# Reading the convolution taps from PSUM, with two more input products on GpSimd, in a graph layer and state-space kernel on one core

## The chip, the core and the metric

The kernel runs on one core of a Trainium2 chip. TensorE (PE in the profile) multiplies matrices into PSUM and loads its weights in parallel (PEld); VectorE (DVE), ScalarE (ACT) and GpSimd (POOL) work on tensors in SBUF, the first two on PSUM too; SyncE (SP) issues transfers. Each engine runs its own list of instructions in order, and the engines meet only at semaphores. The metric is the device time of one execution in microseconds (us), lower is better.

## What is computed

64 sequences of 128 tokens with 256 features pass through a graph layer and a Mamba block, both with a residual. Everything is fp32.

```python
x = x + relu(sum_k Xk @ Wk[k] + bk[k])       # graph layer: Xk = transition @ Xk-1, on layernorm(x)
h = layernorm(x) @ W_fc1.T + b_fc1            # Mamba block, inner width 1024, 16 states
u, z = split(h @ W_in.T)
u = silu(sum(u_pad[:, k:k+L] * conv_w[:, k] for k in range(4)) + conv_b)    # u_pad: 3 zeros ahead
dt, B, C = split(u @ W_xproj.T);  delta = softplus(dt @ W_dt.T + b_dt)
h_t = exp(delta_t * A) * h_t-1 + delta_t * u_t * B_t;  y_t = sum_s h_t * C_t
x = x + fc2(((y + u * D) * silu(z)) @ W_out.T)
```

## The kernel before

**Tiles and stages.** The 64 sequences are 32 pairs; a pair has 256 columns (2 x 128 tokens), and its 1024 inner channels are 8 blocks `j` of 128 partitions. The state recurrence of one pair is cut into 32 units `v`: a unit is two blocks (i = v // 8) times two of the 16 states, 1024 elements for each partition. For each unit, the input product du x B is written to one of eight slots of `st`, by VectorE (`inject`, line 879) or for the units in `POOL_UNITS` by GpSimd (line 388); ScalarE writes the decays exp(delta x A) to one of two PSUM buffers `dec` (four activations, line 467); VectorE runs the recurrence over `st` (`scan_unit`, line 891); GpSimd multiplies by C (`c_product`, line 404); TensorE sums over the states into `y_ps` (`state_sum`, line 699).

**Software pipeline.** Each engine walks the same list: `body(k)` runs units 0 to 31 of pair k, and between them the dense stage of pair k+1 and the graph stage of pairs k+2 and k+3, at fixed unit numbers. Two bodies make one iteration of a hardware loop. Inside a body the order on each engine is written out by hand; nothing is scheduled.

**The dense stage** of pair k+1, by unit. TensorE projects u, two blocks at a time, into the two halves of the one bank `d_ps` (line 739, in `U_STEPS`). One unit later ScalarE copies a block with its bias into a zero-padded SBUF buffer `upad` (line 510) and writes the newest tap's product to `u` (line 513). VectorE then adds the three older taps out of `upad`: 24 operations for a pair (`tap`, line 912), two behind each scan in units 2 to 13. SiLU of u follows in unit 14 (line 526), the x projection in 15 and 16, dt in 18 to 24 (`abs`, `relu`, lines 539 and 540), exp in 22 and 26, ln in 27 (line 550), z in 26 to 29 (lines 751 and 522). SiLU of z is in unit 6 of the pair's own body (line 484). SiLU, ln and exp each need another function table on ScalarE. GpSimd then makes delta (line 370) and delta x u (line 378).

**What holds what.** `d_ps` is one bank for u, x, dt and z: the next projection waits until the last one is read out. In units 2 to 13 `c_product` waits on semaphore `taps` until the two taps behind that unit's scan are done; at two graph operations it waits likewise. `gate` (line 898, in units 2, 10, 18 and 26) reads `y_ps` after the last state sum of a block pair, and TensorE can't start the next block pair's sum (line 695, then 699) before it. `POOL_INJECTS` says after which `c_product` GpSimd makes which unit's input product; `POOL_DELTAS` and `POOL_DUS` do so for lines 370 and 378.

Of the kernel before, what the change touches and what calls it, by code (L numbers as in the profile page):

```python
# [30 lines left out]
UPADS = 6  # L31
# [16 lines left out]
FOLD_OUT = {9: 0, 10: 3, 11: 1, 13: 2}  # L48
# [13 lines left out]
def build(nc, x, adjT, w_inT, w_fc1, w_out, w_fc2T, w_vT, aw, bv, ab, wk, bk, b_fc1, conv_w, conv_b,  # L62
# [5 lines left out]
    with ExitStack() as ctx:  # L68
# [258 lines left out]
        def _(pool):  # L327
            def body(pool, k, p, scan, dense, ends, begins):
                r = 1 - p
                for v in range(U):  # L330
# [61 lines left out]
            def c_product(pool, k, p, v, steps, dense):  # L392
# [3 lines left out]
                if dense and 2 <= v < 2 + (TAPS - 1) * JP:  # L396
                    wait(pool, "taps", (TAPS - 1) * J * (k + 1) + 2 * (v - 2) + 2)
# [14 lines left out]
        def _(act):  # L412
# [60 lines left out]
            def body(act, k, p, scan, dense, ends, begins):  # L473
# [3 lines left out]
                for v in range(U):  # L477
# [11 lines left out]
                    if isinstance(k, int) and k == 0:  # L489
                        fold_wo(act, v)  # L490
# [8 lines left out]
            def dense_act(act, g, r, v):  # L499
                if v - 1 in U_STEPS:  # L500
# [106 lines left out]
        def _(pe):  # L607
# [58 lines left out]
            def body(pe, k, p, scan, dense, ends, begins):  # L666
                r = 1 - p
                for v in range(U):
# [6 lines left out]
                    if isinstance(k, int) and k == 0:  # L675
                        fold_wo(pe, v)
# [359 lines left out]
```

## Time and profile before

| | us |
|---|---|
| median of 3 runs (4177.37 to 4192.95) | 4181.41 |
| the profiled execution's own time | 4176.09 |
| its span, first to last instruction | 4174.3 |
| VectorE busy | 3766.7 (90%) |
| TensorE busy | 3575.7 (86%) |
| GpSimd busy | 3326.2 (80%) |
| ScalarE busy | 2976.9 (71%) |

In the views below a group's row gives source line, engine, operation, what it writes and reads, shapes and count, then busy time in us and mean nanoseconds of one, then the engine's idle time before the group and what ended it. Engines overlap a little from one instruction to the next, so an instruction occupies its engine slightly less than its duration; the distance from one start to the next shows it. Granted TensorE clock over the span was 0.96 of full speed.

### The profile page before, as it was taken

The page shows a single profiled execution, that of the slowest core. Times are in us where ns is not written, and L with a number is a line of the kernel's source. Part 1 is how long each engine was busy: PE and PEld are TensorE (multiplying, and loading weights), DVE is VectorE, ACT ScalarE, POOL GpSimd, SP SyncE. Part 2 cuts the span into 40 slices and gives each one's busy share as a digit, 9 for nine tenths or more (in the row PEclk, how much of TensorE's full clock was granted, in tenths as well). Part 3 has the DMA queues.
Part 4 walks back from the last instruction along what each step waited for, and adds up shares of the span by engine and source line. Part 5 has one row for each costly group of instructions (what it writes and reads, how often), then busy time and mean ns, then how long its engine had stood idle before and what let it go on. Part 6 is the DMA issues. An engine that isn't in the chain of part 4 may idle for free.

```text
span 4174.3 us, 45057 instructions
## 1 busy us (share of the span) xinstructions
PE 3575.7 (86%) x11386; PEld 2016.6 (48%) x11386; DVE 3766.7 (90%) x3219; ACT 2976.9 (71%) x6358; POOL 3326.2 (80%) x1764
## 2 busy tenths in 40 slices
PE   6688889888888888889888888888889888888887
PEld 3454555444545444545444445444545444555443
DVE  0399999999999999999899999999999999999998
ACT  1577777777777777777777777777777777777764
POOL 0287878888888888888888888888878888788888
PEclk9799999999999999999999999999999999999999
DMA  2111001111101111101111101111101111101110
GB/s 96 47 50 53 36 29 43 50 52 52 39 25 44 49 52 52 52 12 43 50 52 52 52 12 44 49 52 52 51 12 43 50 52 52 39 25 43 46 46 8
DMA packets 50716, 183.79 MB, mean 44 GB/s; under 512 B 7339, under 2 KB 33203, under 8 KB 42067
## 3 DMA queue, kind: packets, MB, share of 16 engines
q1 hardware_dynamic: 48880, 174.17, 11.0%
q10 hardware_dynamic: 1636, 7.83, 0.5%
q14 instruction: 182, 1.49, 0.1%
q8 instruction: 18, 0.29, 0.0%
HBM read 164.15 MB, written 17.83 MB: 44 GB/s over the span
## 4 chain that ended last, share of the span: by engine, by line
PE 32%; DVE 23%; ACT 19%; issue 17%; POOL 6%; DVEq 1%; DMA 0%; ACTq 0%; POOLq 0%; SPq 0%
PE y_ps L699 15%; DVE st L891 11%; ACT dec L467 8%; PE d_ps L751 4%; DVE st L879 4%; POOL st L404 4%; DVE u L912 3%; PE y_ps L695 3%; PE d_ps L762 2%; ACT L467 2%; PE d_ps L739 2%; PE d_ps L773 2%; DVE zs L898 2%; ACT delta L550 1%; ACT zs L522 1%
## 5 line engine op out<-in xcount | busy, mean ns | idle before, releaser
L404 POOL TENSOR_TENSOR st<-st,bc 128x1024 f32<-128x1024 f32 x1024 | 2403.4, 2356 | 642.7 <-DVE u L912 373.5
L891 DVE TENSOR_TENSOR_SCAN st<-dec,st 128x1024 f32<-128x1024 f32 x1024 | 2327.5, 2279 | 176.9 <-ACT dec L467 174.9
L467 ACT ACTIVATE dec<-delta,decay 128x254 f32<-128x254 f32 x4096 | 1700.6, 467 | 797.1 <-DVE st L891 791.1
L699 PE MATMUL y_ps<-st,ident 128*128 128x512 f32 x4096 | 2023.1, 624 | 242.3 <-POOL st L404 237.3
L699 PEld LDWEIGHTS y_ps<-st,ident 128*128 128x128 f32 x4096 | 770.2, 197 | 1025.9 <-issue 612.6
L879 DVE TENSOR_TENSOR st<-du,bc 128x1024 f32<-128x1024 f32 x800 | 963.5, 1204 | 36.2 <-ACT du L453 35.9
L388 POOL TENSOR_TENSOR st<-du_sb,bc 128x1024 f32<-128x1024 f32 x224 | 528.6, 2360 | 0.1
L912 DVE SCALAR_TENSOR_TENSOR u<-upad,chan,u 128x256 f32<-128x256 f32 x768 | 392.3, 551 | 6.4 <-ACT u L513 6.4
L695 PE MATMUL y_ps<-u,diag 128*128 128x256 f32 x512 | 157.6, 434 | 209.7 <-DVE zs L898 209.7
L751 PE MATMUL d_ps<-xnT,wxz 128*128 128x256 f32 x1024 | 254.7, 393 | 62.9 <-ACT zs L522 62.2
L751 PEld LDWEIGHTS d_ps<-xnT,wxz 128*128 128x128 f32 x1024 | 198.3, 196 | 161.7 <-ACT zs L522 103.3
L721 PE MATMUL g<-wo,zs 128*128 128x256 f32 x1024 | 248.7, 386 | 0.8 <-DVE zs L898 0.8
L739 PE MATMUL d_ps<-xnT,wxz 128*128 128x256 f32 x1024 | 244.5, 382 | 1.1 <-ACT u L513 0.9
L721 PEld LDWEIGHTS g<-wo,zs 128*128 128x128 f32 x1024 | 196.0, 194 | 98.8 <-issue 76.6
L739 PEld LDWEIGHTS d_ps<-xnT,wxz 128*128 128x128 f32 x1024 | 196.5, 192 | 82.4 <-issue 60.8
L695 PEld LDWEIGHTS y_ps<-u,diag 128*128 128x128 f32 x512 | 91.9, 199 | 287.3 <-DVE zs L898 279.2
L370 POOL TENSOR_TENSOR delta<-delta,relu 128x512 f32<-128x512 f32 x128 | 162.3, 1268 | 35.4 <-ACT delta L550 35.1
L522 ACT ACTIVATE zs<-d_ps,bxz 128x256 f32<-128x256 f32 x256 | 106.5, 466 | 99.6 <-PE d_ps L751 99.6
L510 ACT ACTIVATE upad<-d_ps,bxz 128x256 f32<-128x256 f32 x256 | 120.0, 469 | 71.8 <-PE d_ps L739 71.8
L378 POOL TENSOR_TENSOR du_sb<-delta,u 128x512 f32<-128x512 f32 x128 | 162.6, 1271 | 0.1
L539 ACT ACTIVATE delta<-d_ps,chan 128x256 f32<-128x256 f32 x256 | 120.9, 472 | 41.7 <-PE d_ps L773 40.0
L773 PE MATMUL d_ps<-dbc,rows 32*128 32x256 f32 x512 | 145.0, 402 | 5.1 <-ACT relu L540 5.1
(105 smaller groups left out, 2831.2 us busy)
## 6 DMA issues: line engine op xcount, KB each, us to landing
bc<-bc_dram SPq DMA_DIRECT2D x64, 2048.0 KB, 9.6
xg<-x_dram SPq DMA_DIRECT2D x32, 256.0 KB, 2.8
x_dram<-xg SPq DMA_DIRECT2D x32, 256.0 KB, 2.0
last_x<-x_dram SPq DMA_DIRECT2D x32, 256.0 KB, 2.6
out_dram<-last_x SPq DMA_DIRECT2D x32, 256.0 KB, 2.2
bc<-w_inT_dram ACTq DMA_DIRECT2D x1, 4096.0 KB
adjt<-adjT_dram SPq DMA_DIRECT2D x32, 128.0 KB, 2.5
bc<-w_out_dram ACTq DMA_DIRECT2D x1, 2048.0 KB
```

The lines of the kernel that those rows point to most:

```text
L388: nc.gpsimd.tensor_tensor(st[:, sl, :, :, :], du_sb[:, None, :, :].to_broadcast([P, SU, 2, T]), bc[:, r, 0, SU * q:SU * q + SU, None, :].t ...
L404: nc.gpsimd.tensor_tensor(st[:, sl, :, :, :], st[:, sl, :, :, :], bc[:, p, 1, SU * q:SU * q + SU, None, :].to_broadcast([P, SU, 2, T]), AL ...
L467: a = nc.scalar.activation(dec[:, v % 2, s, j, :].rearrange("p (b t) -> p b t", b=PAIR)[:, :, 1:], delta[:, p, 2 * i + j, :].rearrange("p ...
L695: nc.tensor.matmul(y_ps[:, j, :], diag[:, 2 * i + j, :], u[:, p, 2 * i + j, :], start=(j == 0), stop=False, skip_group_check=True)
L699: mm = nc.tensor.matmul(y_all, ident[:, :], st[:, sl, s, :, :].rearrange("p j t -> p (j t)"), start=False, stop=(q == Q - 1 and s == SU - ...
L721: mm = nc.tensor.matmul(o_ps[:, b, :], zs[:, p, j, b * L:(b + 1) * L], wo[:, j, :], start=False, stop=(j == J - 1), skip_group_check=True)
L739: mm = nc.tensor.matmul(d_ps[:, j % 2, :], wxz[:, c, j * P:(j + 1) * P], xnT[:, r, c, :], start=(c == 0), stop=(c == KC - 1))
L751: mm = nc.tensor.matmul(d_ps[:, j % 2, :], wxz[:, c, INNER + j * P:INNER + (j + 1) * P], xnT[:, r, c, :], start=(c == 0), stop=(c == KC - 1))
L773: mm = nc.tensor.matmul(d_ps[:, j % 2, :], wdt[:, j * P:(j + 1) * P], dbc[0:RANK, :], start=True, stop=True)
L879: nc.vector.tensor_tensor(st[:, sl, :, :, :], du[:, None, :, :].to_broadcast([P, SU, 2, T]), bc[:, p, 0, SU * q:SU * q + SU, None, :].to_b ...
L891: nc.vector.tensor_tensor_scan(h, dec[:, v % 2, :, :, :].rearrange("p s j t -> p (s j t)"), h, 0.0, ALU.mult, ALU.add).then_inc(S["scanned ...
L912: nc.vector.scalar_tensor_tensor(dst, upad[:, j % UPADS, :, m:m + L], chan[:, m, j:j + 1], dst, ALU.mult, ALU.add).then_inc(S["taps"], 1)
```

## The change

The taps no longer read `upad`. They read the projection where TensorE left it, in `d_ps`, and `upad` with its ScalarE copy (8 for a pair) is gone. Since nothing is padded there, a tap that is `late` tokens behind covers 128 - `late` columns of each sequence. The bias of the projection is folded into one constant for a channel (`bconv`), and the first three tokens, for which that is too much, get one correcting addition of 48 elements a partition at the end (`edge`). All six taps of two blocks now stand behind one scan, in units 1, 3, 5 and 7, and the next u projection waits for them (`taps`) and not for ScalarE (`u_biased`).

With it: the wait on `taps` in `c_product` is dropped; u's last projection is in unit 6 instead of 7; SiLU of u in 9 instead of 14; the x projection in 11 and 12 instead of 15 and 16; dt in 14 to 20; exp in 18 and 22; ln in 24; SiLU of z in 3 instead of 6. GpSimd makes nine input products instead of seven (units 4 and 12 are added), VectorE 23 instead of 25. Folding W_out and fc2 into one matrix, done once, moves from the first pair's units to the body before it, and VectorE copies the results.

```diff
-POOL_UNITS = (0, 8, 16, 20, 24, 27, 30)
-POOL_INJECTS = {5: 8, 13: 16, 17: 20, 20: 24, 24: 27, 26: 30}
-POOL_DELTAS = {2: 1, 9: 2, 11: 3}
-POOL_DUS = {4: 1, 12: 2, 18: 3}
+POOL_UNITS = (0, 4, 8, 12, 16, 20, 24, 27, 30)
+POOL_INJECTS = {0: 4, 5: 8, 8: 12, 12: 16, 16: 20, 20: 24, 23: 27, 26: 30}
+POOL_DELTAS = {2: 1, 9: 2, 14: 3}
+POOL_DUS = {4: 1, 11: 2, 18: 3}
...
-U_STEPS = (0, 2, 4, 7)
+U_STEPS = (0, 2, 4, 6)
 Z_STEPS = (26, 27, 28, 29)
-SILU_U, SILU_Z = 14, 6
+X_STEPS = (11, 12)
+DT_STEPS = (14, 16, 18, 20)
+EXP_STEPS = (18, 22)
+LN_STEP = 24
+SILU_U, SILU_Z = 9, 3
...
                 wait(pool, "scanned", U * k + v + 1)
-                if dense and 2 <= v < 2 + (TAPS - 1) * JP:
-                    wait(pool, "taps", (TAPS - 1) * J * (k + 1) + 2 * (v - 2) + 2)
...
                     for j in (2 * i, 2 * i + 1):
-                        nc.scalar.activation(upad[:, j % UPADS, :, TAPS - 1:],
-                                             d_ps[:, j % 2, :].rearrange("p (b t) -> p b t", b=PAIR),
-                                             ACT.Identity, bias=bxz[:, j:j + 1])
                         nc.scalar.activation(u[:, r, j, :], d_ps[:, j % 2, :], ACT.Identity, bias=bconv[:, j:j + 1],
                                              scale=chan[:, TAPS - 1, j:j + 1]).then_inc(S["u_biased"], 1)
...
-                        wait(pe, "u_biased", J * g + 2 * i)
+                        wait(pe, "taps", CONV * g + 6 * i)
...
-            def tap(dve, g, r, v):
-
-                if not 2 <= v < 2 + (TAPS - 1) * J // 2:
-                    return
-                i, m = (v - 2) // (TAPS - 1), (v - 2) % (TAPS - 1)
...
-                    nc.vector.scalar_tensor_tensor(dst, upad[:, j % UPADS, :, m:m + L], chan[:, m, j:j + 1], dst,
-                                                   ALU.mult, ALU.add).then_inc(S["taps"], 1)
+            def conv(dve, g, r, v):
+
+                for i, start in enumerate(U_STEPS):
+                    for n in range(6):
+                        if v == start + 1:
+                            tap(dve, g, r, i, n)
+                if v == U_STEPS[3] + 1:
+
+                    wait(dve, "taps", CONV * (g + 1) - 1)
+                    first = u[:, r, :, :].rearrange("p j (b t) -> p j b t", b=PAIR)[:, :, :, 0:TAPS - 1]
+                    nc.vector.tensor_tensor(first, first, edge[:, :, None, :].to_broadcast([P, J, PAIR, TAPS - 1]),
+                                            ALU.add).then_inc(S["taps"], 1)
+
+            def tap(dve, g, r, i, n):
+
+                m, j, late = n // 2, 2 * i + n % 2, TAPS - 1 - n // 2
+                if m == 0:
+                    wait(dve, "u_biased", J * g + 2 * i + 2)
+                else:
+                    wait(dve, "taps", CONV * g + 6 * i + n - 1)
+                dst = u[:, r, j, :].rearrange("p (b t) -> p b t", b=PAIR)[:, :, late:]
+                src = d_ps[:, j % 2, :].rearrange("p (b t) -> p b t", b=PAIR)[:, :, 0:L - late]
+                nc.vector.scalar_tensor_tensor(dst, src, chan[:, m, j:j + 1], dst, ALU.mult, ALU.add)\
+                    .then_inc(S["taps"], 1)
```

VectorE in the first scanning body, from the scan of unit 2 on before the change, and from the scan of unit 1 on after it. `st<-du,bc` is an input product, `st<-dec,st` a scan, `u<-...` the taps. Before:

```order
L891 SCALAR_TENSOR_TENSOR st<-dec,st 128x1024
L912 SCALAR_TENSOR_TENSOR u<-upad,chan,u 128x256 x2
L879 TENSOR_TENSOR st<-du,bc 128x1024
L891 SCALAR_TENSOR_TENSOR st<-dec,st 128x1024
L912 SCALAR_TENSOR_TENSOR u<-upad,chan,u 128x256 x2
L879 TENSOR_TENSOR st<-du,bc 128x1024
```

After:

```order
L866 SCALAR_TENSOR_TENSOR st<-dec,st 128x1024
L898 SCALAR_TENSOR_TENSOR u<-d_ps,chan,u 128x2x125 x2
L898 SCALAR_TENSOR_TENSOR u<-d_ps,chan,u 128x2x126 x2
L898 SCALAR_TENSOR_TENSOR u<-d_ps,chan,u 128x2x127 x2
L854 TENSOR_TENSOR st<-du,bc 128x1024
L866 SCALAR_TENSOR_TENSOR st<-dec,st 128x1024 x2
L898 SCALAR_TENSOR_TENSOR u<-d_ps,chan,u 128x2x125 x2
```

Twos behind every scan became sixes behind every second one, the first of them a unit earlier; the two scans in a row are units 2 and 3, since unit 4's input product went to GpSimd.

ScalarE at the same place, from the decays of unit 2 on (`dec<-` x4 is one unit's decays; L513, now L500, writes the newest tap; L477 is SiLU of z). Before:

```order
L467 ACTIVATE dec<-delta,decay 128x2x127 x4
L510 ACTIVATE upad<-d_ps,bxz 128x2x128
L513 ACTIVATE u<-d_ps,bconv,chan 128x256
L510 ACTIVATE upad<-d_ps,bxz 128x2x128
L513 ACTIVATE u<-d_ps,bconv,chan 128x256
L467 ACTIVATE dec<-delta,decay 128x2x127 x4
L590 ACTIVATE xn<-g 128x512
```

After:

```order
L460 ACTIVATE dec<-delta,decay 128x2x127 x4
L500 ACTIVATE u<-d_ps,bconv,chan 128x256 x2
L460 ACTIVATE dec<-delta,decay 128x2x127 x4
L577 ACTIVATE xn<-g 128x512
L460 ACTIVATE dec<-delta,decay 128x2x127 x4
L500 ACTIVATE u<-d_ps,bconv,chan 128x256 x2
L477 ACT_TABLE_LOAD
L477 ACTIVATE zs<-zs 128x2048
L460 ACT_TABLE_LOAD
```

The copies to `upad` are gone, and SiLU of z with its two table loads now stands in unit 3, behind the second pair of u writes.

## Rows read from the trace of the kernel before

**Rows 1.** The page, busy time of each engine, share of the span, instructions.
```profile
PE 3575.7 (86%) x11386; PEld 2016.6 (48%) x11386; DVE 3766.7 (90%) x3219; ACT 2976.9 (71%) x6358; POOL 3326.2 (80%) x1764
```
**Rows 2.** Ln, once a pair, whole span, then to 3800 us: ns min/median/max, first and last start.
```profile
L550 ACT ACTIVATE delta<-delta x32: 1910/1911/1912, 177.0 to 4040.1; 128x2048 f32<-128x2048 f32 x32
...
L550 ACT ACTIVATE delta<-delta x29: 1910/1910/1912, 177.0 to 3678.9; 128x2048 f32<-128x2048 f32 x29
```
**Rows 3.** Waits over the span: engine, line, waited for; us in total, times, longest.
```profile
POOL st L404 <- DVE u L912: 373.5, 279, 3.0
PE y_ps L695 <- DVE zs L898: 209.7, 126, 4.2
DVE st L891 <- ACT dec L467: 174.9, 138, 4.3
...
ACT du L453 <- issue: 26.3, 13, 2.3
```
**Rows 4.** Groups of VectorE instructions over the span, by shape.
```profile
L891 DVE TENSOR_TENSOR_SCAN st<-dec,st 128x1024 f32<-128x1024 f32 x1024 | 2327.5, 2279 | 176.9 <-ACT dec L467 174.9
L879 DVE TENSOR_TENSOR st<-du,bc 128x1024 f32<-128x1024 f32 x800 | 963.5, 1204 | 36.2 <-ACT du L453 35.9
L912 DVE SCALAR_TENSOR_TENSOR u<-upad,chan,u 128x256 f32<-128x256 f32 x768 | 392.3, 551 | 6.4 <-ACT u L513 6.4
L898 DVE TENSOR_TENSOR zs<-y_ps,zs 128x512 f32<-128x512 f32 x128 | 87.2, 681 | 42.8 <-PE y_ps L699 42.7
...
L937 DVE TENSOR_TENSOR att<-att,u1T 128x256 f32<-128x256 f32 x32 | 37.8, 1181 | 60.0 <-ACT u1T L575 60.0
```
**Rows 5.** Groups of GpSimd instructions over the span, by shape.
```profile
L404 POOL TENSOR_TENSOR st<-st,bc 128x1024 f32<-128x1024 f32 x1024 | 2403.4, 2356 | 642.7 <-DVE u L912 373.5 <-DVE st L891 145.0 <-DVE xg L958 94.9
L388 POOL TENSOR_TENSOR st<-du_sb,bc 128x1024 f32<-128x1024 f32 x224 | 528.6, 2360 | 0.1
...
L370 POOL TENSOR_TENSOR delta<-delta,relu 128x512 f32<-128x512 f32 x128 | 162.3, 1268 | 35.4 <-ACT delta L550 35.1
```
**Rows 6.** A tap, and the operation of the same form that reads PSUM: min/median/max.
```profile
L912 DVE SCALAR_TENSOR_TENSOR u<-upad,chan,u x768: 451/473/1849, 125.1 to 3993.2; 128x256 f32<-128x256 f32 x192
...
L953 DVE SCALAR_TENSOR_TENSOR x1k<-g,rinv,x1k x64: 469/470/485, 94.7 to 3849.8; 128x256 f32<-128x256 f32 x64
```
**Rows 7.** VectorE in time: start us, us; units 1 and 2 of a pair.
```profile
1316.13 2.28 DVE L891 TENSOR_TENSOR_SCAN st<-dec,st 128x1024 f32<-128x1024 f32 x1
1318.32 1.20 DVE L879 TENSOR_TENSOR st<-du,bc 128x1024 f32<-128x1024 f32 x1
1319.44 0.68 DVE L898 TENSOR_TENSOR zs<-y_ps,zs 128x512 f32<-128x512 f32 x1
1320.04 2.28 DVE L891 TENSOR_TENSOR_SCAN st<-dec,st 128x1024 f32<-128x1024 f32 x1
```
**Rows 8.** GpSimd, then VectorE, in time: two taps behind the scan of unit 6.
```profile
1338.26 2.38 POOL L388 TENSOR_TENSOR st<-du_sb,bc 128x1024 f32<-128x1024 f32 x1
...
1339.13 2.19 DVE L912 SCALAR_TENSOR_TENSOR u<-upad,chan,u 128x256 f32<-128x256 f32 x2
```
**Rows 9.** TensorE in time, around the sum that waits for the gate of unit 2.
```profile
1320.17 1.13 PE L695 MATMUL y_ps<-u,diag 128*128 128x256 f32 x4 [2.43 <-DVE zs L898]
1321.14 1.88 PE L699 MATMUL y_ps<-st,ident 128*128 128x512 f32 x4
1322.86 1.89 PE L739 MATMUL d_ps<-xnT,wxz 128*128 128x256 f32 x8
```
**Rows 10.** ScalarE in time: decays, the newest tap's product, SiLU of z.
```profile
1322.35 1.66 ACT L467 ACTIVATE dec<-delta,decay 128x254 f32<-128x254 f32 x4 [1.73 <-DVE st L891]
...
1326.04 0.57 ACT L513 ACTIVATE u<-d_ps,bconv,chan 128x256 f32<-128x256 f32 x1
...
1336.58 1.28 ACT L484 ACT_TABLE_LOAD   x1
```
**Rows 11.** VectorE in time: the scan of unit 29, behind ln.
```profile
1427.44 2.29 DVE L891 TENSOR_TENSOR_SCAN st<-dec,st 128x1024 f32<-128x1024 f32 x1 [4.31 <-ACT dec L467]
```

More of the change, by code:

```diff
@@ L47 @@
 FOLD_STEP = 16
-FOLD_OUT = {9: 0, 10: 3, 11: 1, 13: 2}
+FOLD_OUT = (1, 3, 5, 7)
+CONV = (TAPS - 1) * J + 1
 PE_LAG = 1
@@ L87, in build @@
         bconv = sb("bconv", [P, J])
+        edge = sb("edge", [P, J, TAPS - 1])
+        part = sb("part", [P, TAPS - 1, J])
         c0 = sb("c0", [P, 2])
@@ L524, in dense_act @@
                 if v == SILU_U:
-                    wait(act, "taps", (TAPS - 1) * (J * g + J))
+                    wait(act, "taps", CONV * (g + 1))
                     nc.scalar.activation(u[:, r, :, :], u[:, r, :, :], ACT.Silu).then_inc(S["silu_u"], 1)
-                if v == 17:
+                if v - 1 == X_STEPS[1]:
                     wait(act, "proj_mm", g + 1)
@@ L674, in body @@
                         fold(pe, v)
-                    if isinstance(k, int) and k == 0:
+                    if dense and not scan:
                         fold_wo(pe, v)
@@ new lines, in conv_constants @@
+            def conv_constants(dve):
+                dve.wait_ge(S["bias_loaded"], 16)
+                for m in range(TAPS - 1):
+                    nc.vector.scalar_tensor_tensor(part[:, m, :], bxz[:, 0:J], -1.0, chan[:, m, :], ALU.mult, ALU.mult)\
+                        .then_inc(S["edge_part"], 1)
+                nc.vector.tensor_tensor(bconv[:, :], bxz[:, 0:J], chan[:, TAPS - 1, :], ALU.mult)\
+                    .then_inc(S["edge_part"], 1)
+                dve.wait_ge(S["edge_part"], 4)
+                nc.vector.tensor_copy(edge[:, :, 2], part[:, 0, :])
+                nc.vector.tensor_tensor(edge[:, :, 1], part[:, 0, :], part[:, 1, :], ALU.add).then_inc(S["edge_part"], 1)
+                nc.vector.tensor_tensor(bconv[:, :], bconv[:, :], chan[:, TAPS, :], ALU.add).then_inc(S["edge_part"], 1)
+                dve.wait_ge(S["edge_part"], 6)
+                nc.vector.tensor_tensor(edge[:, :, 0], edge[:, :, 1], part[:, 2, :], ALU.add).then_inc(S["edge_part"], 1)
+                dve.wait_ge(S["edge_part"], 7)
+                nc.vector.tensor_tensor(bconv[:, :], bconv[:, :], edge[:, :, 0], ALU.subtract)\
+                    .then_inc(S["bconv_made"], 1)
@@ L915, in graph_dve, with fold_wo @@
+            def fold_wo(dve, v):
+                if v - 1 in FOLD_OUT:
+                    m = FOLD_OUT.index(v - 1)
+                    wait(dve, "wo_mm", m + 1)
+                    nc.vector.tensor_copy(wo[:, 2 * m:2 * m + 2, :].rearrange("p j d -> p (j d)"), y_all)\
+                        .then_inc(S["wo_folded"], 1)
             def graph_dve(dve, g, v, late):
@@ L990, in body @@
                     if dense:
-                        tap(dve, k + 1, r, v)
+                        conv(dve, k + 1, r, v)
+                    if dense and not scan:
+                        fold_wo(dve, v)
                     for g, _, ph in steps:
```

74 lines of the change are left out of this document (19 added, 55 removed).

## The prediction, made before the changed kernel had run

> **What bounds the kernel now.** Read the page's busy times first [rows 1]: VectorE leads with 90%. Then the rhythm. Ln runs once a pair, so its starts give the period: (3678.9 - 177.0) / 28 = 125.1 us while all stages run, and (4040.1 - 3678.9) / 3 = 120.4 for the last three [rows 2]. Then the work of a pair on VectorE, by what an instruction occupies (from start to start), not by its duration: scan 2.20, input product 1.12, gate 0.60 [rows 7], in each case 0.08 less than the duration in the groups [rows 4]. A pair has 32 scans (70.4), 25 input products (28.0), 24 taps at 0.551 - 0.08 (11.3), 4 gates (2.4) and some 5 us of graph operations: 117. The other 8 us are waits: for decays 174.9 / 32 = 5.5, for the state sum ahead of a gate 42.7 / 32 = 1.3 [rows 3, 4]. The largest single one is behind ln: scan 29 stands 4.3 us [rows 11]. So VectorE's own work sets the pace, and ScalarE's table functions add to it. GpSimd is busy 3326.2 / 32 = 103.9 us a pair and stands still the rest, 373.5 us in all because it waits for taps [rows 1, 3, 5].
>
> **The change part by part**, for one pair.
>
> *Two input products move*: VectorE -2 x 1.12 = -2.2; GpSimd +2 x 2.32 = +4.6 (2.36 less the overlap) [rows 5], so 108.5 of busy time.
>
> *The taps' source.* Clean taps take 0.473 and the mean is 0.551, the longest 1.849 [rows 4, 6]. The pair of taps behind scan 6 shows why: it took 2.19 instead of about 0.86, and began at 1339.13 while GpSimd's product ran until 1340.64; VectorE got through when GpSimd was done [rows 8]. A tap has two inputs in SBUF. The operation of the same form with its first input in PSUM never did this: 0.469 to 0.485 in 64 instances, while GpSimd works beside it too [rows 6]. So 24 taps cost 24 x 0.39 = 9.4, which is -1.9. That they must be clean is also why the dropped wait in `c_product` costs nothing: it kept GpSimd off the taps.
> The Trainium skill ("VectorE: DVE Perf Modes", the section on the TRN2 errata) speaks against this: its table has a PSUM source at 120 cycles fixed and an SBUF source at 58, at 0.96 GHz. By it an estimate for 24 taps is +1.55 us a pair, some 48 us in all, which would eat most of the gain from the cleaner taps. The rows show 0.470 against 0.473 for the same form and size [rows 6], so the sum doesn't carry it.
>
> *The corrective addition* (48 elements) isn't in the trace. Below, it is a small operation with a wait for the tap ahead, 0.2; above, its two SBUF inputs meet a GpSimd product, 2.4 more. I take 0.3: by the account below GpSimd has just finished unit 7's product then.
>
> *ScalarE* loses 8 copies, 3 us off the path. Ln moves to unit 24, where its 4.5 us (load, function, load back [rows 2, 10]) stand beside three scans, the attention operation and a gate on VectorE. Decays are made up to two units ahead and take 1.66 [rows 10]; so about 4 us may stand between them unnoticed, 6 there. I let the wait behind ln go entirely, and SiLU's in unit 9 too.
>
> *New waits, at the head of each burst.* Before, a tap came two units after its u was written for most blocks; now VectorE wants it in the very unit. Count from the end of scan 0. (a) Unit 1: on GpSimd the input product for unit 0 stands ahead of product 30; where GpSimd sets the pace (below), scan 0 starts when that input is ready and product 30 ends with scan 0, at 0. TensorE's sum of unit 30 (1.7, four starts of 0.43 [rows 9]) and first u projection (1.9) follow, then ScalarE's two blocks (1.0), with the semaphores 4.9; VectorE comes at 3.3: 1.6. (b) Unit 3: the burst of unit 1 ends at 7.3, an input product and the gate of unit 2 follow until 9.0. TensorE holds its sum for that gate, and from the gate's end to the end of the next u projection it takes 1324.75 - 1320.12 = 4.6 [rows 7, 9]; ScalarE writes two blocks in 1.0 [rows 10]: 14.7. VectorE comes at 13.4, since unit 4's input product isn't its own any more: 1.3. (c) Unit 5, behind SiLU of z on ScalarE: 0.2. (d) Unit 7: decays 1.7 and two blocks 1.0 after scan 6, VectorE there after 2.2: 0.6 with the semaphore. Together 3.7, and nothing of the kind before (6.4 us in the whole span [rows 4]). What hides more is only GpSimd's slack.
>
> *First stretch*, end of scan 0 to the graph layer's residual in unit 8: 6 input products 6.7, 8 scans 17.6, 24 taps 9.4, gate 0.6, correction 0.3, three graph operations 1.4, waits 3.7: **39.7**. GpSimd keeps up here.
>
> *Second stretch*, from there to the scan of the next unit 0. GpSimd holds product 8 for that residual (a wait that stays), and then has a closed list: of its 108.5, the units before are 10 products and 2 inputs (27.8) and one delta and one du (2.5); 78.2 remain up to the input product of the next unit 0 (products 30 and 31 come after it and are among the ten). With 0.8 for the attention operation in unit 23, for which product 23 waits as before, **79.1**. VectorE in the same stretch: 17 inputs 19.0, 23 scans 50.6, 3 gates 1.8, graph operations 3.3 (the 5 above less 1.4 and the attention maximum's clean part), attention maximum 1.1 to 3.3 (its mean is 1.18 with 0.4 its own: it too stands behind a GpSimd product, and GpSimd now has its products back to back [rows 4]); with the gate of unit 18, for which product 15 is some 5 us late, 77 to 80. The two are level: neither has much left.
>
> *Sum*: 39.7 + 79.1 + scan 0 2.2 = 121.0. ScalarE's return to the head of the hardware loop, 26.3 / 13 = 2.0 for two pairs [rows 3], was partly hidden; between 0 and 1.0 a pair, 0.6 taken: **121.6 against 125.1, -3.5**. For 29 pairs -101; for the two with less graph work -2.5 each; for the last, which has no taps, -2. The way to the first scan gets the serial bursts (four times u, ScalarE, six taps) and the folding of W_out: between -4 and +8 once, +3 taken. Total -105: 4176.1 - 105 = 4071 for the profiled execution, which lay 5.3 under the median of its runs: 4076.
>
> **The rivals.** *VectorE alone remains the bound.* If GpSimd's lag never reaches TensorE and the gates, its work is 36.0 + 76 + 2.2, with the waits of ScalarE 116.5 a pair: 8.6 x 29 + 8 - 3 = 254 less, **3927**. For it: GpSimd's 108.5 fit into 116.5. Against: they lie unevenly, 79 in the second stretch. *The gain is eaten up.* TensorE, ScalarE and VectorE form a ring through `d_ps` now; if each burst's head waits 0.8 longer than worked out, or TensorE (86% busy, holding 209.7 us for gates already [rows 1, 3]) falls behind in 11 to 20, the period is back near 124.8: **4168**, no difference. *Slower, by the shared access.* Every collision in this trace ended with one GpSimd instruction, because a wait held GpSimd afterwards [rows 8]. Now the correction has no such wait, and the attention maximum meets a queue without gaps. If VectorE doesn't get its turn between two GpSimd instructions, each further one costs 2.32 and through the scan and the gate behind it GpSimd's own next product too; from two a pair on (4.6, against 3.5) it is slower than before; with three, 128.6 and **4290**. The Trainium skill ("SBUF — State Buffer", two separate sides) calls this access a lock held for the whole instruction, whoever starts first; of the turn after it, it says nothing, nor does a row here.
>
> **How the numbers follow.** The account as summed: 0.52, its own range 4035 to 4125 (one us a pair either way and the bounds of the prologue). VectorE alone, or most of the way there: 0.22. Eaten up: 0.20. Slower: 0.06. A tenth left out on each side gives 3985 to 4150. A measurement of this kernel tells 0.5% (21 us) from no change: faster 0.86, same 0.08, slower 0.06; the third case is mostly on the slow side of the boundary, but its milder half is still faster.
>
> **What would show it.** Taps of 0.47 with hardly any spread, and no wait of GpSimd for taps. A period of ln near 121.6. VectorE waiting for ScalarE's u writes some 3 to 4 us a pair, at units 1 and 3 above all. No wait of 4 us behind ln. GpSimd busy near 89 to 90% of the period, without a gap from unit 8 on, and gates of unit 18 that wait for TensorE. The correction near 0.2 if no product is under way. The forecast is wrong if the taps are slower than 0.5, if the bursts' heads cost more than 6 us a pair, or if the attention maximum or the correction stand for two GpSimd instructions or more.

## The result

| | kernel before | changed kernel |
|---|---|---|
| time, median of 9 and of 8 runs | 4177.4 us | 4202.0 us |
| lowest and highest | 4168.95, 4192.95 | 4196.68, 4203.42 |
| profiled execution: time, span | 4176.1, 4174.3 | 4201.6, 4199.6 |
| granted TensorE clock, mean | 0.961 | 0.947 |

The ratio is 1.0053, 95% interval 1.0040 to 1.0066: a little slower, where 2.4% faster was forecast. A ninth run of the changed kernel took 8748.7 us, at a mean granted clock of 0.456, and is left out.

The page's busy times and the groups of VectorE and GpSimd instructions after the change answer to [rows 1, 4, 5]:

```profile
PE 3628.5 (86%) x11386; PEld 2059.3 (49%) x11386; DVE 3672.1 (87%) x3197; ACT 2875.8 (68%) x6098; POOL 3444.9 (82%) x1828
```
```profile
L866 DVE TENSOR_TENSOR_SCAN st<-dec,st 128x1024 f32<-128x1024 f32 x1024 | 2314.5, 2276 | 83.0 <-ACT dec L460 80.5 <-POOL st L393 1.8
L854 DVE TENSOR_TENSOR st<-du,bc 128x1024 f32<-128x1024 f32 x736 | 884.5, 1202 | 47.1 <-ACT du L446 40.3 <-PE y_ps L681 6.8
L898 DVE SCALAR_TENSOR_TENSOR u<-d_ps,chan,u 128x254 f32<-128x254 f32 x256 | 110.3, 472 | 0.0
L898 DVE SCALAR_TENSOR_TENSOR u<-d_ps,chan,u 128x250 f32<-128x250 f32 x256 | 110.1, 472 | 155.6 <-ACT u L500 154.5
...
L873 DVE TENSOR_TENSOR zs<-y_ps,zs 128x512 f32<-128x512 f32 x128 | 86.8, 678 | 14.1 <-PE y_ps L681 14.1
L949 DVE TENSOR_TENSOR att<-att,u1T 128x256 f32<-128x256 f32 x32 | 71.2, 2226 | 58.6 <-ACT u1T L562 58.6
L935 DVE BATCH_NORM_STATS2 bstat<-xg 128x6 f32<-128x256 f32 x128 | 47.8, 415 | 94.6 <-DMA xg<-x_dram 94.5
```
```profile
L407 POOL TENSOR_TENSOR st<-st,bc 128x1024 f32<-128x1024 f32 x1024 | 2398.4, 2355 | 556.7 <-DVE st L866 365.3
```

The first line says that the change did what it was made for: VectorE is busy 94.6 us less, GpSimd 118.7 more, ScalarE 101.1 less. The last columns say why that did not count. The taps wait 154.5 us for ScalarE's `u` (L500), where the waits had been 6.4 [rows 4]; the statistics on x (L935, `bn_stats`) wait 94.5 us for a load, 11.1 before (all 11.1 in the first 150 us; a pair had none); the input products wait 47.1 instead of 36.2. That is 242 us more. Less are the waits for decays by 94 (174.9 [rows 3], now 80.5), those of the gates by 29 (42.8 [rows 4], now 14.1) and the work by 95: 218. The difference, 24, is that of the spans, 25.

Ln still gives the period. Line L537, whole span, answers to [rows 2]:

```profile
L537 ACT ACTIVATE delta<-delta x32: 1909/1911/1913, 175.5 to 4062.4; 128x2048 f32<-128x2048 f32 x32
```

Below, "period" is the distance of one pair's scan 0 from the next one's, as a mean over pairs 3 to 28, from the scans' start times; "work" is what VectorE's instructions occupy in it, from start to start, and "waits" is the rest. Before: 125.0 = 117.6 + 7.4. After: 126.2 = 114.6 + 11.6. The first stretch (end of scan 0 to the residual in unit 8) went from 35.1 to 41.0, the second from 87.6 to 82.9.

### The profile page after: what moved, and what is told of

Its sections match the earlier page's. It is cut to its first block and busy times, and to the rows that moved or that the text cites. A ratio compares the mean times of both kernels' runs of the same rounds, so it can differ in the third digit from the quotient of the medians.

```text
span 4199.6 us, 44407 instructions
## 1 busy us (share of the span) xinstructions
PE 3628.5 (86%) x11386; PEld 2059.3 (49%) x11386; DVE 3672.1 (87%) x3197; ACT 2875.8 (68%) x6098; POOL 3444.9 (82%) x1828
## 5 line engine op out<-in xcount | busy, mean ns | idle before, releaser
L407 POOL TENSOR_TENSOR st<-st,bc 128x1024 f32<-128x1024 f32 x1024 | 2398.4, 2355 | 556.7 <-DVE st L866 365.3
L866 DVE TENSOR_TENSOR_SCAN st<-dec,st 128x1024 f32<-128x1024 f32 x1024 | 2314.5, 2276 | 83.0 <-ACT dec L460 80.5
L681 PE MATMUL y_ps<-st,ident 128*128 128x512 f32 x4096 | 2036.9, 626 | 196.0 <-POOL st L407 192.9
L681 PEld LDWEIGHTS y_ps<-st,ident 128*128 128x128 f32 x4096 | 769.9, 198 | 1019.5 <-issue 576.3
L854 DVE TENSOR_TENSOR st<-du,bc 128x1024 f32<-128x1024 f32 x736 | 884.5, 1202 | 47.1 <-ACT du L446 40.3
L393 POOL TENSOR_TENSOR st<-du_sb,bc 128x1024 f32<-128x1024 f32 x288 | 678.9, 2357 | 0.1
L898 DVE SCALAR_TENSOR_TENSOR u<-d_ps,chan,u 128x250 f32<-128x250 f32 (+2 forms) x768 | 309.0, 471 | 155.6 <-ACT u L500 154.5
L677 PE MATMUL y_ps<-u,diag 128*128 128x256 f32 x512 | 170.7, 464 | 220.9 <-DVE zs L873 220.9
L701 PE MATMUL g<-wo,zs 128*128 128x256 f32 x1024 | 295.1, 440 | 0.8 <-DVE zs L873 0.8
L701 PEld LDWEIGHTS g<-wo,zs 128*128 128x128 f32 x1024 | 224.3, 222 | 104.9 <-issue 70.7
L719 PE MATMUL d_ps<-xnT,wxz 128*128 128x256 f32 x1024 | 247.0, 385 | 3.8 <-DVE u L898 3.6
L677 PEld LDWEIGHTS y_ps<-u,diag 128*128 128x128 f32 x512 | 104.7, 222 | 291.0 <-DVE zs L873 278.8
L719 PEld LDWEIGHTS d_ps<-xnT,wxz 128*128 128x128 f32 x1024 | 199.5, 195 | 93.9 <-issue 53.9
L500 ACT ACTIVATE u<-d_ps,bconv,chan 128x256 f32<-128x256 f32 x256 | 128.9, 553 | 135.3 <-PE d_ps L719 135.3
L751 PE MATMUL d_ps<-dbc,rows 32*128 32x256 f32 x512 | 146.3, 405 | 2.0 <-ACT relu L527 2.0
```

The costliest lines, as they stand in the source:

```text
L393: nc.gpsimd.tensor_tensor(st[:, sl, :, :, :], du_sb[:, None, :, :].to_broadcast([P, SU, 2, T]), bc[:, r, 0, SU * q:SU * q + SU, None, :].t ...
L407: nc.gpsimd.tensor_tensor(st[:, sl, :, :, :], st[:, sl, :, :, :], bc[:, p, 1, SU * q:SU * q + SU, None, :].to_broadcast([P, SU, 2, T]), AL ...
L677: nc.tensor.matmul(y_ps[:, j, :], diag[:, 2 * i + j, :], u[:, p, 2 * i + j, :], start=(j == 0), stop=False, skip_group_check=True)
L681: mm = nc.tensor.matmul(y_all, ident[:, :], st[:, sl, s, :, :].rearrange("p j t -> p (j t)"), start=False, stop=(q == Q - 1 and s == SU - ...
L701: mm = nc.tensor.matmul(o_ps[:, b, :], zs[:, p, j, b * L:(b + 1) * L], wo[:, j, :], start=False, stop=(j == J - 1), skip_group_check=True)
L719: mm = nc.tensor.matmul(d_ps[:, j % 2, :], wxz[:, c, j * P:(j + 1) * P], xnT[:, r, c, :], start=(c == 0), stop=(c == KC - 1))
```

## Where the time stands in the changed kernel

**The head of the burst in unit 3.** VectorE's timeline of pair 11, from scan 1 on (start and duration in us, line, operation, count, then the idle time ahead and what ended it):

```profile
1583.72 2.39 DVE L898 SCALAR_TENSOR_TENSOR u<-d_ps,chan,u 128x250 f32<-128x250 f32 x6
1586.03 1.21 DVE L854 TENSOR_TENSOR st<-du,bc 128x1024 f32<-128x1024 f32 x1
1587.16 0.68 DVE L873 TENSOR_TENSOR zs<-y_ps,zs 128x512 f32<-128x512 f32 x1
1587.76 4.46 DVE L866 TENSOR_TENSOR_SCAN st<-dec,st 128x1024 f32<-128x1024 f32 x2
1596.43 2.42 DVE L898 SCALAR_TENSOR_TENSOR u<-d_ps,chan,u 128x250 f32<-128x250 f32 x6 [4.22 <-ACT u L500]
```

TensorE in the same place:

```profile
1587.89 2.08 PE L677 MATMUL y_ps<-u,diag 128*128 128x256 f32 x4 [4.79 <-DVE zs L873]
1589.76 3.62 PE L681 MATMUL y_ps<-st,ident 128*128 128x512 f32 x4
1593.17 2.09 PE L719 MATMUL d_ps<-xnT,wxz 128*128 128x256 f32 x8
```

and the same instructions in the kernel before (diagonal L695, sum L699, projection L739):

```profile
1571.54 1.13 PE L695 MATMUL y_ps<-u,diag 128*128 128x256 f32 x4 [2.03 <-DVE zs L898]
1572.50 1.88 PE L699 MATMUL y_ps<-st,ident 128*128 128x512 f32 x4
1574.22 1.89 PE L739 MATMUL d_ps<-xnT,wxz 128*128 128x256 f32 x8
```

The gate (L873) now stands behind six taps, so TensorE stands 4.79 us for it and not 2.03. Then the diagonal takes 2.08 instead of 1.13 and the sum 3.62 instead of 1.88. The granted clock, in stretches of 2 us (length, busy us and count of PE, PEld, DVE, ACT, POOL, then PEclk, DMA), says why:

```profile
1584.00:1586.00 2.00, 0.00 (x0) 0.00 (x0) 2.00 (x6) 2.00 (x5) 2.00 (x2) 1.00 0.00 0
1586.00:1588.00 2.00, 0.11 (x1) 0.11 (x1) 2.00 (x4) 0.01 (x1) 1.54 (x1) 0.69 0.00 0
1588.00:1590.00 2.00, 2.00 (x5) 1.65 (x6) 2.00 (x2) 0.00 (x0) 0.00 (x0) 0.50 0.00 0
```

TensorE was at its lower level, 1.2 GHz, when the gate released it (it had fallen at 1586.7). From the start of the diagonal to the end of the projection it took 7.4 us here, against 4.6 before. The pairs alternate: odd ones stand 4.79 us and take 7.2 to 7.4, even ones stand 2.68 and take 6.1 to 6.2. The wait in unit 3 is 4.1 to 4.3 and 2.8 to 3.0 by turns, 3.5 us in the mean. Take off what the three groups last beyond 4.6, and 1.3 to 1.4 are left in either kind of pair: the clock is 2.2 of the 3.5. The run e10_stats_z below shows the same without that subtraction.

**The load in unit 12.** VectorE, and then the queue of SP:

```profile
1503.00 1.20 DVE L854 TENSOR_TENSOR st<-du,bc 128x1024 f32<-128x1024 f32 x1
1507.03 0.75 DVE L935 BATCH_NORM_STATS2 bstat<-xg 128x6 f32<-128x256 f32 x2 [2.84 <-DMA xg<-x_dram]
```
```profile
1504.28 0.39 SPq L263 DMA_DIRECT2D xg<-x_dram  x1
```

The load of x may start when ScalarE has normalised the old x (its pass ended at 1504.0), and the data are used some 2.8 us after the issue. VectorE comes at 1504.2. Before, taps behind the scans ahead of it and unit 12's own input product on VectorE filled that time; the change took both away, and the wait, none in a pair before, is 2.85. With that input product back on VectorE, in e4 below, it is 1.4; with the taps behind the scans and without the input product, in e5, it is 0, so the taps alone had covered it. GpSimd's list stands still with it (1.4 a pair), since scan 12 is behind the statistics.

**Scan 0.** It starts 2.6 us after GpSimd's input product for it (3.3 before), by turns 0.3 and some 5 us. VectorE waits for ScalarE ahead of it: 1.8 us a pair for the decays of unit 31, 0.2 for those of unit 0 and 1.0 for the copy of delta x u (L446). With z projected earlier, in e7 and e12 below, these waits and the delay are gone.

## The experiments

Ratios are to the kernel before, run beside each on the same chip, with the 95% interval. "Head 3" is the wait of the burst in unit 3, "x load" that of the statistics on x, at scan 12 (behind it in the kernels with e2's edit, where 0.3 of the wait is `bn_aggr`'s for `bn_stats` and not the load's); period, waits and these are us a pair. They are read from the profiled execution, whose time lies up to 14 us from the median: 4138.9 for e1 and 4150.0 for e2, both the lowest of their four.

| kernel | median | ratio | period | waits | head 3 | x load |
|---|---|---|---|---|---|---|
| changed kernel | 4202.0 | 1.0053 [1.0040, 1.0066] | 126.2 | 11.6 | 3.5 | 2.85 |
| e1_gate | 4149.3 | 0.9925 [0.9909, 0.9942] | 123.9 | 9.4 | 0.5 | 2.75 |
| e2_stats | 4163.6 | 0.9957 [0.9941, 0.9974] | 124.5 | 9.9 | 3.2 | 0.9 |
| e3_both | 4105.0 | 0.9819 [0.9803, 0.9835] | 122.8 | 8.7 | 0.5 | 0.8 |
| e4_pool7 | 4246.1 | 1.0142 [1.0119, 1.0165] | 127.8 | 12.2 | 2.2 | 1.4 |
| e5_before9 | 4237.8 | 1.0138 [1.0106, 1.0170] | 127.3 | 8.7 | 0 | 0 |
| e7_z | 4111.7 | 0.9844 [0.9822, 0.9865] | 123.0 | 8.3 | 0.5 | 0.9 |
| e8_att | 4108.0 | 0.9832 [0.9812, 0.9852] | 122.8 | 9.7 | 0.5 | 0.7 |
| e12_z_only | 4207.5 | 1.0068 [1.0051, 1.0084] | 126.4 | 11.7 | 3.0 | 2.8 |
| e10_stats_z | 4145.7 | 0.9916 [0.9900, 0.9933] | 124.1 | 9.4 | 3.1 | 0.9 |
| e11_eight | 4140.0 | 0.9898 [0.9881, 0.9914] | 123.9 | 8.8 | 2.8 | 0.3 |
| e13_swap | 4127.6 | 0.9862 [0.9846, 0.9879] | 123.8 | 9.2 | 0.5 | 2.6 |
| e14_swap_stats | 4081.8 | 0.9752 [0.9736, 0.9768] | 122.4 | 8.2 | 0.5 | 0.8 |

### The two new waits, one by one and together

e1_gate moves the previous pair's last gate ahead of the first six taps:

```diff
-                        elif v % Q == 2 and has_previous(k):
-                            gate(dve, k - 1, r, JP - 1)
                         scan_unit(dve, k, p, v)
+                        if v == 1 and has_previous(k):
+                            gate(dve, k - 1, r, JP - 1)
```

> The changed kernel, with the gate of the previous pair put behind scan 1, ahead of the first six taps, instead of behind them in unit 2. Theory A (the burst holds back that gate, TensorE stands 5 us for it, its clock drops to half, the second u projection is late and VectorE stands 3.5 us in unit 3): the wait in unit 3 falls below 1 us, no half clock at the start of a pair, period 126.2 -> about 123.5, time about 4120. Rival B (the ring through d_ps costs this whatever the order): the wait in unit 3 stays near 3.5, time 4190 to 4205. Rival C (GpSimd's load of nine units sets the pace): the wait goes, but turns up later in the pair, 4195 to 4205.

TensorE in pair 11 of e1_gate (diagonal L677, sum L681, projection L719):

```profile
1564.76 1.13 PE L677 MATMUL y_ps<-u,diag 128*128 128x256 f32 x4 [1.33 <-DVE zs L873]
1565.73 1.88 PE L681 MATMUL y_ps<-st,ident 128*128 128x512 f32 x4
1567.45 1.89 PE L719 MATMUL d_ps<-xnT,wxz 128*128 128x256 f32 x8
```

The waiting is 1.33, the durations are those of the kernel before, and the wait in unit 3 fell from 3.5 to 0.5. Theory A's mechanism came out and nearly its period (123.9 for 123.5), in a profiled execution 63 us shorter than that of the changed kernel; the median gained 53 us and not some 80. Part of the gain is spent at once: the gate now waits for its own sum (1.06 a pair).

e2_stats leaves the order of the taps and issues the statistics behind the scan of unit 12:

```diff
                     for g, _, ph in steps:
-                        graph_dve(dve, g, ph, 0)
+                        if not (scan and ph == 2):
+                            graph_dve(dve, g, ph, 0)
...
                     for g, _, ph in steps:
+                        if scan and ph == 2:
+                            graph_dve(dve, g, ph, 0)
                         graph_dve(dve, g, ph, 1)
```

> The changed kernel, with the two statistics operations on the freshly loaded x put behind the scan of unit 12 instead of ahead of it. Theory A (VectorE stands 2.9 us there for the load of x, which the taps and the input product of unit 12 had covered): the wait falls to 0.7 or less, 31 x 2.2 = 68 us less, 4130. Rival C (GpSimd, already 3 us late there, sets the pace): given back at the gate of unit 18 or the next unit 0, 4190 to 4200.

The statistics' wait in the whole span, e2_stats against 94.5 above:

```profile
DVE bstat L935 <- DMA xg<-x_dram: 31.5, 32, 5.9
```

63 us of waiting went and 38 us of time, not the 68 of theory A: the rest came back as `bn_aggr`'s wait (0.3 a pair) and as waits for decays, 0.9 a pair in unit 17 and 2.5 instead of 1.8 in unit 31, where ScalarE is the next to be late. TensorE still stands 4.79 us in every second pair here, but in 7 of these 13 pairs its clock is full when the gate releases it and falls within the chain, which then takes 6.3. e3_both has both edits.

> Both of the moves above together. Theory A: the gains add, about 4.5 us a pair, 4060. Rival C: GpSimd becomes the bound; the pair can't get below what GpSimd has to do from unit 8 on, and the second move gives nothing more than the first, 4120 or above.

53 + 38 = 91, measured 97: the gains add, but from smaller terms than expected, and 4105 is far from the 4060 of theory A. The two waits explain the loss against the kernel before, and more. Both are a matter of order: the taps read the same PSUM bank in e3_both, and GpSimd has the same nine units.

### The halves of the change apart

e4_pool7 is the changed kernel with the old tables of GpSimd (`POOL_UNITS`, `POOL_INJECTS`, `POOL_DELTAS`, `POOL_DUS`); e5_before9 is the kernel before with the new ones.

> The changed kernel with the seven input products on GpSimd of before (25 on VectorE), all else as changed. Theory A: units 4 and 12 of VectorE's input products come back just where it stands anyway (behind scan 3 of the burst that waits for u, and ahead of the statistics that wait for x), so 2.2 us more work cost nothing: 4195 to 4205, with both waits some 1.1 us shorter. Rival C (GpSimd's load is what cost the gain): clearly faster than the changed kernel, 4130 or less.

> The kernel before with nothing changed but GpSimd's tables: nine input products (units 4 and 12 too), taps out of upad as before. It parts the two halves of the change. Theory A (the harm is in the order of the bursts and in the cover of the load of x, not in GpSimd's load): VectorE has 2.24 us less work in stretches where it never waits, and the taps behind scans 11 and 12 still cover the load: 4177 - 31 x 2.2 = 4110, at most 1 us a pair given back, so 4110 to 4140. Rival C (GpSimd's load): its products come late at the gate of unit 18 and unit 0, 4165 or more.

Neither expectation held. Each half alone is 1.4% slower than the kernel before, the two together 0.5%. For e5 the group of the taps says why; e5_before9, and the minimum, median and maximum of one tap:

```profile
L912 DVE SCALAR_TENSOR_TENSOR u<-upad,chan,u 128x256 f32<-128x256 f32 x768 | 504.0, 696 | 6.4 <-ACT u L513 6.4
```
```profile
L912 DVE SCALAR_TENSOR_TENSOR u<-upad,chan,u x768: 451/474/1847, 122.8 to 4054.4; 128x256 f32<-128x256 f32 x192
```

The median tap is unchanged and the mean rose from 551 [rows 4] to 696 ns: 196 taps last longer than 600 ns, 101 before, and each of these ends 0.28 us after a GpSimd instruction does. In the changed kernel 611 of the 768 taps start while a GpSimd instruction runs, and the longest takes 480 ns. In e5 the rise is 112 us in all, more than the 72 us (2 x 1.12 x 32) that the two products save. Besides, ln's wait grew from 3.5 to 4.3 and the gate of unit 18 waits 2.4 instead of 0.7.

In e4 the head in unit 3 and the load are 1.3 and 1.5 us shorter, more than the 1.1 expected of each. But the gate of unit 18 waits 3.4, where it waited 0.1 in the changed kernel. TensorE in pair 11 of e4_pool7 (sum L681, dt L751, transposes of the graph layer L766), two stretches with the clock, and the gate on VectorE:

```profile
1670.26 2.92 PE L681 MATMUL y_ps<-st,ident 128*128 128x512 f32 x4 [2.23 <-POOL st L407]
1673.11 2.07 PE L751 MATMUL d_ps<-dbc,rows 32*128 32x256 f32 x4
1675.12 1.11 PE L766 MATMUL g<-ident,xn 128*128 128x128 f32 x4
1676.02 2.87 PE L681 MATMUL y_ps<-st,ident 128*128 128x512 f32 x4
```
```profile
1672.00:1674.00 2.00, 2.00 (x4) 0.80 (x3) 2.00 (x2) 0.50 (x2) 2.00 (x2) 0.50 0.99 426
1674.00:1676.00 2.00, 2.00 (x7) 1.26 (x7) 0.66 (x1) 0.70 (x2) 2.00 (x2) 0.50 0.31 131
```
```profile
1678.93 0.69 DVE L873 TENSOR_TENSOR zs<-y_ps,zs 128x512 f32<-128x512 f32 x1 [4.27 <-PE y_ps L681]
```

The clock again: TensorE stands 2.23 us for a product of GpSimd, runs at its lower level, and the gate waits for the sum at the end of that chain. Between the start of scan 15 and this gate the clock is low for 5.1 us a pair, against 0.5 in the changed kernel (2.7 in the kernel before, 4.6 in e5). So reading PSUM is what makes the nine products affordable, as the prediction said; that the new order without them is slower still is a chain at the low clock in another place, not VectorE's 2.2 us of work.

### What holds scan 0

e7_z adds to e3_both an earlier z projection (`Z_STEPS = (22, 23, 25, 27)`), so that ScalarE makes the decays of units 31 and 0 in time. e8_att adds to e3_both a wait in `c_product`: GpSimd holds product 22 and not 23 for the attention matrix, so that the attention maximum runs by itself.

> The changed kernel with gate and statistics moved (e3_both, 4105), and z projected in units 22, 23, 25 and 27 instead of 26 to 29. Theory D (in units 26 to 31 TensorE has a sum of 1.7 and a z projection of 1.7 in every unit, plus two graph products of 0.9, more than VectorE's units last; ScalarE stands for z, makes the decays of unit 31 late, and VectorE stands 2.65 us there and 1.4 in unit 0): the wait in unit 31 falls below 1 us, 31 x 1.5 to 2.5 us less, 4030 to 4060. Rival E (the wait in unit 31 comes from the order on ScalarE, two z blocks and two graph copies between decays, or from GpSimd's products being 4 us late there): it stays above 2 us, 4095 to 4115.

> e3_both with GpSimd held for the attention maximum one product earlier (product 22 instead of 23 waits until it is done), so that it doesn't meet a GpSimd product. The maximum takes 1.66 us of VectorE there, 0.35 when clean. If VectorE is the bound (theory A): 1.3 us a pair less, 4065. If GpSimd's lag matters more (rival C): product 22 starts some 2 us later than it could, the products after it are late, and the wait in unit 31 and 0 grows by as much: 4105 to 4140.

Both edits did at their place what they should, and both times are those of the rivals (E and C). In e7 scan 0 starts 0.03 us after GpSimd's product instead of 3.5; in e8 the maximum takes 0.40 and not 1.58 in the mean. Neither moved the time (4112 and 4108 against 4105; the intervals overlap). In e7 the gate behind scan 1 waits 3.3 instead of 0.8: GpSimd's products 30 and 31 come after that input product, and TensorE's sum and the gate wait for them. In e8 the same gate waits 1.8 and that of unit 26 0.9: GpSimd stands 2.0 us for the attention matrix, and its later products come later.

e12_z_only is the z projection alone in the changed kernel, e10_stats_z with the statistics too, e11_eight is e10 with eight units on GpSimd (12 goes back to VectorE).

> The changed kernel with z projected in units 22, 23, 25 and 27 and nothing else moved. In the changed kernel scan 0 starts 2.6 us after GpSimd's input product for it, where the forecast had 0. Theory D (TensorE's z projections in units 26 to 29 make ScalarE late, and ScalarE makes the decays of units 31 and 0 late): that distance falls to 0.1, and the pair gets up to 2.6 us shorter, 4130 to 4160. Rival F (with scan 0 earlier, GpSimd's products 30 and 31 come later against it, and the heads of the bursts and the gate behind them take the time back): 4185 to 4205.

> e7_z with the gate back in unit 2 behind the burst, that is, the changed kernel with statistics and z moved. In e7_z the gate in unit 1 stands 3.3 us for GpSimd's product 31 and the sum of it. Theory G (once scan 0 follows GpSimd's input product at once, GpSimd's list from unit 8 on, 80 us, is the bound, and the six taps should stand ahead of the gate, to fill the time until product 31 is summed): the gate's wait goes, the first stretch falls from 40.7 to 38 to 39 us, 4040 to 4075. Rival A (the late gate halves TensorE's clock again as in the changed kernel, and the head of the burst in unit 3 costs 3 us): 4110 or more.

> e10_stats_z with the input product of unit 12 back on VectorE: GpSimd has eight. Theory G (GpSimd's list is the bound from unit 8 on): 2.3 us less there, 1.1 us more on VectorE, which has a wait of about 1 us in unit 13 to put it in: 15 to 40 us below e10_stats_z. Rival A (VectorE's work is the bound again): 20 to 35 us above e10_stats_z.

e12: scan 0 is on time, but the head of unit 1 waits 3.0, and the time is that of the changed kernel, as rival F said (2 us above its 4205). e10 gained 56, the statistics' part and some 18 more, not what theory G expected; heads of 2.0 and 3.1 took the rest, and the low clock was back at the gate, as rival A said. e11 gained 6 more, no more than the spread allows, against 15 to 40 by theory G.

In two pairs of e10 between 3 and 28 the clock happened to stay at full speed through that chain. TensorE, then the head on VectorE, in pair 17:

```profile
2311.76 1.13 PE L677 MATMUL y_ps<-u,diag 128*128 128x256 f32 x4 [2.76 <-DVE zs L873]
2312.73 1.88 PE L681 MATMUL y_ps<-st,ident 128*128 128x512 f32 x4
2314.44 1.89 PE L719 MATMUL d_ps<-xnT,wxz 128*128 128x256 f32 x8
```
```profile
2317.50 2.42 DVE L898 SCALAR_TENSOR_TENSOR u<-d_ps,chan,u 128x250 f32<-128x250 f32 x6 [1.42 <-ACT u L500]
```

The order is that of the changed kernel and TensorE stood 2.76 us, but the chain takes 4.6 and the head waits 1.42 (1.34 in pair 24). In the other pairs the chain takes 6.0 to 7.6 and the head 2.7 to 4.5. So the clock makes the difference between the prediction's 1.3 and some 3 us.

In the order of the changed kernel, then, scan 0's delay is no cost of its own: what starts earlier there waits at the next head.

### The order on TensorE instead of VectorE

If the head in unit 3 waits only because the projection is queued on TensorE behind the sum that waits for the gate, then the gate need not move. e13_swap issues the projection of unit 2 ahead of the sum of unit 0; e14_swap_stats adds e2's edit.

```diff
                     if dense:
                         dense_pe(pe, k + 1, r, v, ends)
+                    if scan and dense and v == PE_LAG + 1:
+                        state_sum(pe, k, p, 0)
...
+                        if dense and v == PE_LAG:
+                            continue
                         if v >= PE_LAG:
                             state_sum(pe, k, p, v - PE_LAG)
```

> The changed kernel with one exchange on TensorE: in unit 2 of a scanning body that also has a next pair, the second u projection is issued ahead of the state sum of unit 0 instead of behind it, so it no longer stands behind the wait for the previous pair's gate. VectorE's order is that of the changed kernel: six taps, then the gate. Theory A (the head of the burst in unit 3 waits because the projection stands behind that gate on TensorE): from the end of the burst in unit 1 the projection takes 1.9 at full clock and 3.6 at half, ScalarE 1.0, so u is there after 3.3 to 5.0; VectorE comes after an input product, the gate and two scans, 6.1. The wait of 3.5 us in unit 3 falls under 0.4 at either clock, with no gate wait in its place (the other way, the gate moved ahead, still paid 1.06 in unit 2 for the gate and 0.49 in unit 3): period 126.2 - 3.0, time 4100 to 4135. Rival B (the lost time is the low clock itself and not the order): the sum, now later and still at half clock, holds the next projections in units 4 and 6 or the state sums that free the slots of `st`, and the head waits come back in unit 5 or 7 or at GpSimd's products: time 4165 to 4205.

> The same exchange on TensorE, together with the statistics on x issued behind the scan of unit 12 instead of ahead of it. By theory A both gains stand side by side, as they did with the gate moved (4105): 4202 - 85 - 39 or somewhat less, since the gate's own wait is not paid: 4060 to 4100, the period 121.8 to 122.8. By rival B: 4125 to 4165, the gain of the statistics alone. If the exchange alone gains and the pair gains no more than the better of the two, GpSimd's closed list behind unit 8 is what both ran into: 4100 to 4125.

TensorE in pair 11 of e13_swap (projection L723, diagonal L681, sum L685), then VectorE's scans and the burst:

```profile
1562.24 1.99 PE L723 MATMUL d_ps<-xnT,wxz 128*128 128x256 f32 x8 [3.06 <-DVE u L902]
1564.07 1.03 PE L681 MATMUL y_ps<-u,diag 128*128 128x256 f32 x4
1564.93 1.88 PE L685 MATMUL y_ps<-st,ident 128*128 128x512 f32 x4
```
```profile
1563.83 4.46 DVE L870 TENSOR_TENSOR_SCAN st<-dec,st 128x1024 f32<-128x1024 f32 x2
1568.78 1.64 DVE L902 SCALAR_TENSOR_TENSOR u<-d_ps,chan,u 128x250 f32<-128x250 f32 x4 [0.49 <-ACT u L500]
```

TensorE waits for the taps alone, is released before the gate runs, and has the projection done at 1564.2, four us ahead of VectorE. The 0.49 that is left, a little over the 0.4 expected, is ScalarE's order: the decays of unit 4 stand ahead of the `u` writes and wait for scan 2. Theory A's numbers came out in both, 4127.6 in 4100 to 4135 and 4081.8 in 4060 to 4100. The clock is still at its lower level for 12.7 us a pair in e13 (12.0 in the changed kernel), 5.6 of it between the starts of scans 8 and 10, 2.3 each behind the starts of scans 23 and 26, and the time is 74 us shorter all the same: it counts where it stands between a late release and a waiting VectorE.

e14_swap_stats is the best version, 2.5% faster than before, and close to the prediction's 4076. It is not the same sum, though. Its period is 122.4: first stretch 37.8 (39.7 forecast), second 82.3 (79.1), scan 0 2.3. The second has GpSimd's list at the forecast's length (79.1) and then some 3.1 us until scan 0 starts.

## Why the prediction was wrong

**The work: right.** Taps 0.471 to 0.473 (0.47), VectorE's work 114.6 a pair (36.0 + 76 + 2.2 = 114.2), products and input products on GpSimd 2355 and 2357 ns, the first scan 4.8 us later (+3 taken), no wait of GpSimd for taps, none behind ln (0.5 a pair is left, in unit 23), none behind SiLU of u. The correction takes 0.207, at the lower bound: the 0.3 was fair. The attention maximum has a mean of 2226 ns (1181 [rows 4]); the sum allowed for it. It waits for at most one GpSimd instruction and not for two. The table of the Trainium skill ("VectorE: DVE Perf Modes", the TRN2 errata), with its longer PSUM access, would have given, as an estimate from its two figures, 1.55 us more for 24 taps; the trace disagrees, 471 to 473 ns for a source of 250 to 254 columns in PSUM, 473 for 256 in SBUF [rows 6].

**The head of the burst in unit 3: the step that failed first.** The prediction had the right chain, gate, sum, projection, `u`, and put it at 1.3. It took 4.6 us for the TensorE part from rows at full clock [rows 9]. It had itself put six taps ahead of that gate, but asked only when VectorE would come, not at which clock TensorE would then run. The part is 6.1 to 7.4 at the lower level, and the head 3.5, 2.2 us a pair more than put; in the two pairs of e10 with the full clock it is 1.42 and 1.34, so the order and the other terms of that sum were right. With the gate or the projection moved (e1, e13) the head is 0.5 and the time 53 and 74 us less. Unit 5's and 7's are at their terms (0.1 for 0.2, 0.5 for 0.6). Unit 1's is 0.6 for 1.6, because scan 0 is late and TensorE has that time; where it is not, in e12, it is 3.0. All heads together are 4.8 for 3.7, and the first stretch is 41.0 for 39.7.

**GpSimd's closed list: the second.** Its length was right (79.1 in e14, where nothing breaks it). In the changed kernel it is 80.3, because VectorE stands for the load of x and scan 12 with it. The prediction named what hides ScalarE's ln; it did not ask what the removed taps and the removed input product had hidden. The load has no term in the sum. In the trace of before it showed no wait in any pair, since the taps covered it; moving its reader (e2) gave 38 us back.

**Scan 0: the third.** The sum let it start with GpSimd's product. It starts 2.6 later, as it had started 3.3 later before. The term was left out although the trace of before shows it; only 0.6 a pair was taken, for the head of the hardware loop. e7 and e12 show that it cannot simply be added either: without it the loss appears at the gates or at unit 1.

Together, 1.3 + 1.2 + 2.6 = 5.1; less the 0.6 just named and with 0.1 of rounding, the 4.6 us between 121.6 and 126.2.

**The rivals.** "The gain is eaten up" was the right one in kind: the ring through `d_ps`, with heads longer than worked out, 4168 at a chance of 0.20. The heads are 1.1 us a pair longer in the mean, and the measured time is 34 beyond that rival, near the 38 that the load cost. "Slower, by the shared access" did not happen. "VectorE alone" is far off: no version of the changed kernel has less than 8 us of waits a pair.

## What to carry to other kernels

When work leaves an engine, list what ran beside it: a load, a function, a product whose wait was short only because of it; and look at what was queued ahead of each wait whose place in the order changes. When a consumer moves next to its producer, write down everything that stands between them on every engine's own queue; here an exchange of two blocks on TensorE was worth 74 us. And when a matmul's duration goes into a sum, read the granted clock beside it, and give the sum for both levels where the standing ahead of it changes: here 4.6 and up to 7.4 us.

## What the runs showed of the hardware

- TensorE's granted clock fell to one half (1.2 GHz) while it stood 4.79 and 2.68 us in the changed kernel, and the same three groups of matmuls then took 7.4 and 6.2 us instead of 4.6. In e2 it stood 4.79 us in 13 pairs, and in 7 of them the clock fell only after the release (6.3 us). It stayed at full speed, 2.4 GHz, after 3.06 us (e13, pair 11) and 2.76 us (e10, pair 17), and in 23 of the pairs 3 to 28 of the kernel before, where it stood 0.8 to 2.4 us; in the other three it fell within the chain. The length of the standing alone doesn't decide it, and what does is left open.
- A tap with its first input in PSUM takes the time of one from SBUF (472 and 473 ns), and none of 768 was held by GpSimd (longest 480 ns). One with both inputs in SBUF went from a mean of 551 to 696 ns when GpSimd had two more products, at an unchanged median: the mean of such a group against its median shows the collisions.
